# Cross-attention scores as paired 64-row matmuls in two row groups of the array, in place of stacked 128-row operands filled by DMA

## What is computed

```python
x:   (32, 64, 512)      # 32 batches, 64 queries, DIM = 512, HEADS = 16, hd = 32
ctx: (32, 512, 384)     # 512 keys, CTX_DIM = 384
q = (layernorm(x) @ Wq).reshape(B, N, HEADS, hd).transpose(0, 2, 1, 3)
k = (context @ Wk).reshape(B, M, HEADS, hd).transpose(0, 2, 1, 3)
v = (context @ Wv).reshape(B, M, HEADS, hd).transpose(0, 2, 1, 3)
scores = jnp.einsum('bhid,bhjd->bhij', q, k) * hd ** (-0.5)
scores = jnp.where(context_mask[:, None, None, :], scores, max_neg)
out = jnp.einsum('bhij,bhjd->bhid', softmax(scores), v)
x = x + out.transpose(0, 2, 1, 3).reshape(B, N, DIM) @ Wo
```

## Time and profile before

| | |
|---|---|
| runs before, us | 1577.88, 1574.34, 1575.95; median 1575.95 |
| profiled execution, its own time | 1576.93 us |
| its span, first to last instruction | 1575.1 us |
| cross-attention stage, score matmuls (L253) | first at 85.6 us, last at 1008.8 us |
| L253 matmuls | 256 with `qz_h` and 256 with `qz_l` |
| transfers into `KK` | 512, 64 rows by 2 KB each, median 2.3 us from issue to landing |
| transfers within `qz_h` | 128, median 2.3 us |
| mean granted TensorE clock | 0.977 of full speed |

### The profile page before, as it was taken

One profiled execution on the slowest core, in us unless ns is written; L12 is line 12 of the kernel. 1 busy time (PEld: TensorE's weight loads), 2 busy tenths in 40 slices (PEclk: granted clock), 3 DMA queues, 4 the chain that ended last, 5 costly groups with the idle time before them and its releaser, 6 DMA issues. The chain is left out here.

```text
span 1575.1 us, 30765 instructions
## 1 busy us (share of the span) xinstructions
PE 1485.3 (94%) x8760; PEld 1222.4 (78%) x8760; DVE 1063.1 (67%) x2551; ACT 1047.7 (67%) x2279; POOL 762.9 (48%) x873
## 2 busy tenths in 40 slices
PE   6899999999999999999999999668999997699998
PEld 5788888888888888888888888546777776478686
DVE  4367777777777777777777777747887887942323
ACT  5378888888888888888888888724444544623231
POOL 7454554655655645545545544243333332357342
PEclk9999999999999999999999999889999997799999
DMA  6154454453454444444444443310000000223231
GB/s 222 28 148 117 102 134 104 103 138 98 110 132 102 111 127 109 108 122 112 121 114 105 127 115 78 121 47 2 2 2 2 1 1 1 94 77 97 67 141 60
DMA packets 90400, 141.83 MB, mean 90 GB/s; under 512 B 14177, under 2 KB 26849, under 8 KB 90337
## 3 DMA queue, kind: packets, MB, share of 16 engines
q1 hardware_dynamic: 90336, 141.00, 33.4%
HBM read 61.25 MB, written 4.19 MB: 42 GB/s over the span
## 5 line engine op out<-in xcount | busy, mean ns | idle before, releaser
L336 ACT ACTIVATE prob<-prob,rinv 128x512 f32<-128x512 f32 x256 | 185.5, 725 | 111.2 <-DVE rinv L408 111.2
L383 DVE CUSTOM_DVE_ANT_0 prob<-psum,mbias 128x512 f32<-128x512 f32 x256 | 176.5, 689 | 74.5 <-PE psum L253 61.1
L332 ACT ACTIVATE prob<-prob,nmx 128x512 f32<-128x512 f32 x256 | 185.5, 725 | 6.5
L289 PE MATMUL psum<-PT,V_hl 128*128 128x256 f32 x1024 | 185.8, 304 | 0.4 <-DVE PT L403 0.4
L403 DVE TENSOR_TENSOR PT<-psum,PT 128x512 fp32r<-128x512 f32 x256 | 177.1, 692 | 9.4 <-ACT PT L321 1.5
L275 PE MATMUL psum<-ident,prob 128*128 128x128 f32 x1024 | 153.5, 272 | 9.7 <-ACT prob L336 9.7
L275 PEld LDWEIGHTS psum<-ident,prob 128*128 128x128 f32 x1024 | 127.0, 140 | 45.6 <-ACT prob L336 12.5
L503 POOL CAST qz_h<-tok 32x128 fp32r (+1 forms) x256 | 73.3, 286 | 177.4 <-PE psum L253 124.2
L236 PE MATMUL psum<-ctx_h,wk_h 128*128 128x512 f32 x384 | 151.8, 395 | 1.7 <-DVE k_lo L303 1.7
L399 DVE TENSOR_REDUCE o_main<-psum 32x64 f32<-32x128 f32 x512 | 143.4, 280 | 13.1 <-PE psum L289 1.1
L236 PE MATMUL psum<-ctx_h,wk_l 128*128 128x512 f32 x384 | 152.2, 396 | 0.0
(11 more groups left out here) (199 smaller groups left out, 3591.9 us busy)
## 6 DMA issues: line engine op xcount, KB each, us to landing
KK<-k_hi SPq DMA_DIRECT2D x256, 128.0 KB, 2.3
KK<-k_lo SPq DMA_DIRECT2D x256, 128.0 KB, 2.3
ctx_r<-in_ctx SPq DMA_DIRECT2D x32, 768.0 KB, 4.9
w_r<-in_L_ffn_W SPq DMA_DIRECT2D x64, 256.0 KB, 2.8
qz_h<-qz_h SPq DMA_DIRECT2D x128, 64.0 KB, 2.3
xres<-in_x SPq DMA_DIRECT2D x16, 256.0 KB, 2.7
out<-tok SPq DMA_DIRECT2D x16, 256.0 KB, 3.1
tok<-in_x SPq DMA_DIRECT2D x3, 1024.0 KB, 11.9
```

What stands on the lines that cost most here:

```text
L289: ins = pe.matmul(PV_bank[x % 2][:, 0:2 * P], V_hl[:, x % SPT // PAIRS, kt, x % PAIRS, :, :].rearrange("p a b -> p (a b)"), PT[:, x % 4, k ...
L332: act.activation(prob[:, j % 2, :], prob[:, j % 2, :], ACT.Exp, bias=nmx[:, c], scale=-1.0, accum_out=rsum[:, c]).then_inc(s_ex, 1)
L336: act.activation(prob[:, j % 2, :], prob[:, j % 2, :], ACT.Copy, scale=rinv[:, c]).then_inc(s_pn, 1)
L383: dve.tensor_tensor_reduce(prob[:, j % 2, :], S_bank[j % 2][:], mbias[:, j // PAIRS, :], 1.0, 3.0e38, ALU.add, ALU.min, nmx[:, c]).then_in ...
```

## The change

Keys stay where they were projected: `k_h` and `k_l` hold all four key tiles of a batch, 128 rows each, and `KK`, the staging buffers and all transfers into `KK` and within `qz_h` are gone, with their semaphores. `qz_h` and `qz_l` lose the axis that told the two stackings apart. An even slot computes the scores of its own pair and of the next one: pair `p` sits in rows 0 to 63, pair `p + 1` in rows 64 to 127 of the same key tile. Each of the three products is now a matmul of its own, of 64 rows, for each pair, with `tile_position` 0 or 64: six matmuls for two slots. Odd slots compute no scores. The even slot waits for `s_mx` at least `s`, the minimum of the slot just before. Constants of the feed-forward stage move to the end of SBUF and `o_h`, `o_l` of the self-attention to another region; these moves add no instruction.

```diff
+        k_h, k_l = m("k_h", [P, DT, SK], F32R), m("k_l", [P, DT, SK], F32R)
-        KK = m("KK", [P, PAIRS, SK], F32R)
-        qz_h, qz_l = m("qz_h", [P, 2, DT, 2, SQ], F32R), m("qz_l", [P, 2, DT, 2, SQ], F32R)
+        qz_h, qz_l = m("qz_h", [P, DT, 2, SQ], F32R), m("qz_l", [P, DT, 2, SQ], F32R)
...
+        HALF = [slice(0, P // 2), slice(P // 2, P)]
...
         def pe_slot(pe, g, j, first=False, last=False, tail=False):
...
-            if not tail:
+            if not tail and p % 2 == 0:
                 if p % 4 == 0:
                     pe.wait_ge(s_qz, g * (BPG * 16) + b * 16 + (p // 4 + 1) * 8)
-                    pe.wait_ge(s_qd[p // 4], (g * BPG + b) * 32 + 32)
-                if p % 2 == 0:
-                    pe.wait_ge(s_kk[p // 2 % 2], moved(g, b * TILES + p) + 64)
-                if not (first and j < 2):
-                    pe.wait_ge(s_mx, s - 1)
-
-                for q in (qz_h, qz_l):
-                    ins = pe.matmul(S_bank[j % 2][:], q[:, p % 2, p // 2, :, :].rearrange("p a b -> p (a b)"),
-                                    KK[:, p, :], start=(q is qz_h), stop=(q is qz_l))
-                ins.then_inc(s_S, 1)
+                pe.wait_ge(s_KVl, g * SPT + b * TILES + p + 1)
+                if not (first and j == 0):
+                    pe.wait_ge(s_mx, s)
+
+                for i, (q, k) in enumerate(((qz_h, k_h), (qz_h, k_l), (qz_l, k_h))):
+                    for h, rows in enumerate(HALF):
+                        ins = pe.matmul(S_bank[h][:], q[rows, p // 2, :, :].rearrange("p a b -> p (a b)"),
+                                        k[rows, p // 2, :], start=(i == 0), stop=(i == PRODUCTS - 1),
+                                        tile_position=(h * (P // 2), 0))
+                        if i == PRODUCTS - 1:
+                            ins.then_inc(s_S, 1)
...
         def act_kv(act, g, k):
             act.wait_ge(s_KV, g * SPT + k + 1)
-            if KV_ORDER[k % TILES][0] == "K" and not (isinstance(g, int) and g == 0 and k < 4):
-                act.wait_ge(s_kk[k // 2 % 2], moved(g, k))
...
         def sp_tile(sp, g, first, last):
             if not last:
                 sp_context(sp, g, 2, False)
-            sp_queries(sp, g, 0, 1)
-            sp_keys(sp, g, 6)
-            sp_keys(sp, g, 8)
-            sp_queries(sp, g, 1, 0)
-            sp_keys(sp, g, 10)
-            sp_keys(sp, g, 12)
```

More of the change, by code:

```diff
@@ L143, in perceiver_layer @@
         ctx_end = m.at
-        k_hi, k_lo = m("k_hi", [P, 2, SK], F32R), m("k_lo", [P, 2, SK], F32R)
         o_main, o_low = m("o_main", [P, 2, 2, SQ], F32), m("o_low", [P, 2, 2, SQ], F32)
@@ L156, in perceiver_layer @@
         s_qz = sem("p2_qz")
-        s_qd = [sem(f"p2_qd{i}") for i in range(2)]
-        s_kk = [sem(f"p2_kk{i}") for i in range(2)]
         s_mb = sem("p2_mb")
@@ L172, in perceiver_layer @@
         KV_ORDER = [(kind, t) for t in range(DT) for kind in "KV"]
-        UPPER, LOWER = slice(0, P // 2), slice(P // 2, P)
+        HALF = [slice(0, P // 2), slice(P // 2, P)]
         PRODUCTS = 3
@@ L189, in high_part @@
             kind, t = KV_ORDER[k % TILES]
-            return V_hl[:, (k // TILES) % 2, t, :, 0, :] if kind == "V" else k_hi[:, t % 2, :]
+            return V_hl[:, (k // TILES) % 2, t, :, 0, :] if kind == "V" else k_h[:, t, :]
         def low_part(k):
             kind, t = KV_ORDER[k % TILES]
-            return V_hl[:, (k // TILES) % 2, t, :, 1, :] if kind == "V" else k_lo[:, t % 2, :]
+            return V_hl[:, (k // TILES) % 2, t, :, 1, :] if kind == "V" else k_l[:, t, :]
         def kv_source(k):
@@ L200, in kv_source @@
             return b.rearrange("p (a n) -> p a n", a=PAIRS) if KV_ORDER[k % TILES][0] == "V" else b
-        def moved(g, k):
-            return (g * BPG + k // TILES) * (64 * DT // 2) + k % TILES // 4 * 64
         def pt_half(j, low):
@@ L422, in sp_context @@
             sp.dma_start(mask8[:, b % BPG, :], mask[bass.ds(n, 1), :].broadcast_to([P, SK])).then_inc(s_mraw[b % BPG], 16)
[L424 to L441, removed]
         def sp_tile(sp, g, first, last):
@@ L457, in sp_tile @@
                 sp_context(sp, g, 3, False)
[L458 to L464, removed]
         def pool_ctx(pool, g, b, first):
@@ L490, in pool_q @@
                     rows = slice(r * HD, (r + 1) * HD)
-                    src, dst = qt[rows, t, b, :], qz_h[rows, r // 2, t, r % 2, :]
+                    src, dst = qt[rows, t, b, :], qz_h[rows, t, r % 2, :]
                     if low or r:
@@ L500, in pool_q @@
                     if low:
-                        ins = pool.tensor_tensor(qz_l[rows, r // 2, t, r % 2, :], src, dst.bitcast(F32), ALU.subtract)
+                        ins = pool.tensor_tensor(qz_l[rows, t, r % 2, :], src, dst.bitcast(F32), ALU.subtract)
                     else:
@@ L598, in _ @@
                 sp_context(sp, 0, 1, True)
-                sp_queries(sp, 0, 0, 0)
             @block.gpsimd
@@ L785, in _ @@
             def _(sp):
-                for k in range(0, AHEAD, 2):
-                    sp_keys(sp, 0, k)
                 tiles(sp, lambda g, first, last: sp_tile(sp, g, first, last))
@@ L859, in perceiver_layer @@
         ST = B * KEEP // P
-        m = Map(nc, end2)
+        const_at = nc.sbuf_usable_end - 7 * 1024
+        assert const_at >= end2
+        m = Map(nc, const_at)
         b1_sb, b2_sb = m("b1_sb", [P, FF], F32), m("b2_sb", [P, D], F32)
@@ L886, in perceiver_layer @@
         k_T = m("k_T", [P, DT, P], F32)
+        o_h, o_l = m("o_h", [P, DT, BPG, SQ], F32R), m("o_l", [P, DT, BPG, SQ], F32R)
         assert m.at <= xn_at, (m.at, xn_at)
@@ L892, in perceiver_layer @@
         mx3, rc3 = m("mx3", [P, HEADS], F32), m("rc3", [P, 2, HEADS], F32)
-        o_h, o_l = m("o_h", [P, DT, BPG, SQ], F32R), m("o_l", [P, DT, BPG, SQ], F32R)
         assert m.at <= ctx_at, (m.at, ctx_at)
@@ L1298, in perceiver_layer @@
         y_sb = m("y_sb", [P, 4, D], F32)
-        assert m.at <= end2, m.at
+        assert m.at <= const_at, (m.at, const_at)
         SC = ST // 4
```

## The result

| | before | changed |
|---|---|---|
| median of the runs, us | 1576.91 (1574.34 to 1577.92, 4 runs) | 1593.97 (1592.50 to 1595.31, 4 runs) |
| ratio to before | | 1.011, 95% interval 1.0092 to 1.0129 |
| profiled execution / span | 1576.93 / 1575.1 | 1592.50 / 1590.7 |
| a tile of the cross-attention stage | 58.39 | 59.44 |

The change makes the kernel 17.1 us slower, 1.1%.

What follows compares the result with a forecast made beforehand. TensorE's issue time was taken as the bound; 0.684 us of pairs plus 0.395 per visit minus 0.91 gave +0.166 per pair of slots, times 125 +20.8 us on 1575.95, 1596.7, stated as 1596.5, range 1586 to 1606.

Steps and rivals of the forecast that it cites:

- The bound: Cross-attention stage: TensorE's issue time sets the pace, busy 199.68 of 200 us, two slots taking 6.9 us.
- A pair costs one matmul: Scores: two 64-row matmuls in different array halves take one matmul's 0.228 us, saving 0.226 us per pair of slots.
- The visit costs 0.395: Scores: switching to 64-row matmuls and back costs 0.198 us at entry and 0.198 at exit, once per pair of slots.
- +0.166 per pair of slots: Cross-attention on TensorE: 0.684 + 0.395 - 0.91 us; over 125 pairs, +20.8 us.
- The rest, at nothing: Removed key and query transfers, ScalarE's key-buffer wait, GpSimd's small operations and memory moves: no effect on time.
- The new wait: Even slot's scores wait for VectorE's minimum of the slot just before; 1.7 us of slack, so no delay.
- ScalarE gains room, its round wouldn't matter: Cross-attention: ScalarE's 3.53 us round is close to TensorE's 3.45 slot, but TensorE's mean slot grows by 0.08.
- The first rival's price: Switching to 64-row matmuls costs nothing: 0.226 us saved per pair of slots, 28 us in all, 1548; chance 0.05.

Runs made afterwards that it cites:

- a_light: The changed kernel with ScalarE's normalization shortened from 512 to 128 columns of each row, part of the computation left out; 1593.2 us, ratio 1.0109, tile 59.44.
- a_full: The changed kernel with six full-height score matmuls of 128 rows per two slots, zeros in the queries' other 64 rows, no 64-row mode; 1628.7 us, ratio 1.0329.
- a_split: The changed kernel with each visit to the 64-row matmuls cut in two, same matmuls, twice the switches; 1643.8 us, ratio 1.0434.
- a_one: The changed kernel with only the product of high queries and high keys, one pair of matmuls per visit; 1575.6 us, ratio 0.9999, tile 58.34.
- b_wo: The kernel before, with slot 7's output projection moved behind the first three of that slot's nine projection matmuls; 1572.65 us, ratio 0.9962, tile 58.04.
- a_dma: The changed kernel with the 512 key transfers put back as copies that nothing reads; 1598.9 us, ratio 1.0128, tile 59.44.
- a_halves: The changed kernel with the six score matmuls reordered, three products of the lower half, then three of the upper; 1595.0 us, ratio 1.0137, tile 59.49.

## Why the prediction was right, and where it was off

**The bound**: right. TensorE's issue order sets the stage; a_light shows it for the changed kernel.

**A pair costs one matmul**: right, and a_full shows the size. I took 0.228 us for a pair of 512 columns; the starts 602.00 and 602.24 show 0.24 (0.236 on average), and what a pair of slots grew by, less the visit, leaves 0.233. What I added to the columns, read off pairs of 256 columns and the full-height scores, was too small for pairs of 512: 0.015 per pair of slots, 2 us in all.

**The visit costs 0.395**: right. Its four parts stand in the timeline, a_split measures 0.39, and a_full, without the change of height, has none of them. The rows of three other places had given it, with other lines and other shapes, before the kernel ran.

**+0.166 per pair of slots**: measured 0.18, so 125 pairs are 22.5 us instead of 20.8.

**The rest, at nothing**: this step missed a term. I listed the idle time of matmuls, found 9.7 us at the transposes and took TensorE's stream for unbroken. It wasn't: in slot 7 of tiles 2 to 15 the start of the output projection lagged by 0.27 and its load was uncovered. The wait stood in a row that the prediction doesn't use, in the kernel before's list of waits for weight loads:

```profile
PEld psum L265 <- DVE o_main L399: 7.0, 13, 0.6
```

In the changed kernel it is gone, and 14 x 0.38 = 5.3 us came back. 22.5 - 5.3 = 17.2, measured 17.1. The two errors, 1.7 us too little and 5.3 too much, partly cancel. That 1596.5 lay only 2.5 us off is in part luck: the median before, over all four runs, is 1.0 above the one that the forecast started from. In the same step the prediction counts 16 GpSimd operations per half batch of queries; there are eight, the same before and after, so nothing hangs on it.

**The new wait**: right, TensorE doesn't wait at the scores.

**ScalarE gains room, its round wouldn't matter**: right in direction. I noted that its 3.53 us round was close to the 3.45 of a TensorE slot and let it be. In a_one that round is the limit, 58.34 us for 16 slots, 3.65 each with slot 7's output projection in the mean.

**The first rival's price**: wrong. I gave a kernel without cost of switching 28 us and said that ScalarE would cap it. a_one takes more than that off TensorE (two pairs, 0.47 us per visit) and ends level with the kernel before. Had the switch been free, TensorE's tile would have been 8 x 0.39 = 3.1 us below 59.44, 56.3, under the 58.3 at which a_one stopped, and the time by my estimate a_one's 1576, no change, not 1548. No run has a free switch, and b_wo's 58.04 shows that the floor can move a little. I priced the mechanism on one engine while the next one stood level with it.

## What to carry to other kernels

Before matmuls are packed into row groups inside a stream of full-height matmuls, count the visits: each costs 0.39 us here, 1.7 matmuls of 512 columns, so a visit must save more than that, and splitting one doubled the price (a_split). Moving the keys with DMA cost the stage nothing here: with and without the 512 transfers beside a full TensorE a tile took 59.44 us (a_dma). Before pricing a gain on the bounding engine, look how close the next engine's round is, and look for TensorE's waits at its weight loads too: the gap of 0.27 us at the output projection showed only there and in the distance between starts.

## What the runs showed of the hardware

Two halves of the array each take their own matmuls in order, but not in the program's common order: with three lower products ahead of three upper ones, both halves started at 603.06 and kept step, and the order was worth 0.05 us a tile (59.49 and 59.44). The Trainium skill, page "TensorE: Matmul & The Clock Gate", Part 3, "The mechanism", says that matmuls start and end in program order; a_halves shows starts out of that order, and the measurement decides. So the last matmul in the program need not stand for both halves. In this kernel the last of each half counts the semaphore; no run here tries a single count.

The cost of a change of height is nearly the same into 64 rows (0.09 more than the usual step, and 0.10 at the next) and out of them (0.09 and 0.11), over the visits of the changed kernel's stage, and it is not visible as idle time: from 400 to 600 us TensorE was busy all 200 us in the changed kernel, in a_split and in a_halves.
